# A rotated tile loop, maxima written by ScalarE, and row work moved across the ends of the attention and the FFN

## The reference, cut to what matters

```
def _L1_attn_ref(x, Wq, Wk, Wv, Wo, bo):           # 16 heads of 8, no mask
    s = einsum('bhtd,bhsd->bhts', q, k) / sqrt(8)
    m = max(s, axis=-1, keepdims=True)
    e = exp(s - m)
    out = einsum('bhts,bhsd->bhtd', e, v) / (sum(e, -1) + 1e-8)
    return out @ Wo.T + bo

def _L1_ffn_ref(x, ...):                           # DEPTH = 6
    for i in range(DEPTH):                         # 16 heads of 64, windows of 32 rows
        x = attn_layer(shift_tokens(x), Wqkv[i], q_scale[i], k_scale[i], Wo[i]) + x
        x = ffn_layer(shift_tokens(x), ln_g[i], ln_b[i], W1[i], b1[i], W2[i], b2[i]) + x
    return x
# attn_layer: q, k, v = split(x @ Wqkv); q, k = l2norm; rotary; local_attention
#             (softmax over the 64 keys of this and the last window); out @ Wo
# ffn_layer:  (x - mean) / sqrt(var + 1e-5) * g + b; a, gate = split(xn @ W1 + b1)
#             a * gelu(gate) @ W2 + b2
x = x + _L1_attn_ref(xn, ...) + _L1_ffn_ref(xn, ...)
```

## Time and profile before

| | us |
|---|---|
| median of three runs | 5288.02 (5263.25 to 5299.2) |
| the profiled execution | 5284.67 |
| its span | 5282.9 |
| PE, DVE, ACT, POOL busy in the span | 4393.2, 3444.4, 2413.4, 2446.8 |

### The profile page before, as it was taken

The page is one execution under the profiler, slowest core; times in us unless marked ns, Lnnn a source line. Parts: engine busy times, 40 slices in busy tenths (PEclk is TensorE's granted clock), DMA queues, the critical chain, the costliest instruction groups (busy, mean ns, idle before and its releaser), DMA issues. The chain is left out here.

```text
span 5282.9 us, 166221 instructions
## 1 busy us (share of the span) xinstructions
PE 4393.2 (83%) x69377; PEld 2783.1 (53%) x69377; DVE 3444.4 (65%) x5635; ACT 2413.4 (46%) x3236; POOL 2446.8 (46%) x3490
## 2 busy tenths in 40 slices
PE   3556548888799988999889998899988999889997
PEld 2333312322466655666556665566655666556664
DVE  6655656666477756777567775677756777467775
ACT  3434425556344443444444454444534445344453
POOL 1000021110567735666257772666726777176670
PEclk8788868888899999999899999999989999899998
DMA  0000011110222212222122221222202222022220
GB/s 28 0 0 0 0 35 41 44 48 30 65 71 71 71 42 57 71 71 71 34 61 70 69 74 31 67 71 71 70 26 73 70 68 74 25 71 71 71 69 17
DMA packets 187582, 273.42 MB, mean 52 GB/s; under 512 B 39248, under 2 KB 81616, under 8 KB 186192
## 3 DMA queue, kind: packets, MB, share of 16 engines
q1 hardware_dynamic: 186960, 263.67, 18.8%
HBM read 39.25 MB, written 8.39 MB: 9 GB/s over the span
## 5 line engine op out<-in xcount | busy, mean ns | idle before, releaser
L1331 ACT ACTIVATE ls_r<-PS 128x1024 f32<-128x1024 f32 x192 | 196.5, 1023 | 1065.6 <-PE PS L1209 1065.6
L1410 DVE TENSOR_TENSOR ls_a<-PS,TC 128x1024 f32<-128x1024 f32 x384 | 467.9, 1220 | 327.4 <-ACT ls_r L1331 326.7
L1209 PE MATMUL PS<-WQ,ls_xsT 128*128 128x512 f32 x768 | 458.0, 727 | 158.3 <-issue 146.2
L1110 POOL TENSOR_TENSOR ls_a<-ls_a,ls_q 128x1024 f32<-128x1024 f32 x192 | 453.1, 2360 | 241.9 <-DVE ls_q L1415 241.9
L1420 DVE TENSOR_REDUCE ls_ss<-ls_r 128x16 f32<-128x1024 f32 x384 | 466.4, 1214 | 94.2 <-ACT ls_r L1356 94.2
L1415 DVE TENSOR_TENSOR ls_q<-PS,TS 128x512 f32<-128x512 f32 x768 | 491.6, 682 | 0.0
L1130 POOL TENSOR_TENSOR ls_a<-ls_a,ls_q 128x1024 f32<-128x1024 f32 x192 | 454.8, 2369 | 0.0
L1266 PE MATMUL PS<-WO,ls_r 128*128 128x128 f32 x3072 | 404.1, 286 | 58.3 <-ACT ls_r L1359 58.3
L864 DVE TENSOR_REDUCE mxs<-PS 128x2 f32<-128x1024 f32 x256 | 307.6, 1221 | 215.2 <-PE PS L739 213.3
L1266 PEld LDWEIGHTS PS<-WO,ls_r 128*128 128x128 f32 x3072 | 367.0, 196 | 104.9 <-ACT ls_r L1359 104.9
L1217 PE MATMUL PS<-WQ,ls_xsT 128*128 128x512 f32 x768 | 394.7, 639 | 20.9 <-DVE ls_a L1410 20.9
(11 more groups left out here) (238 smaller groups left out, 8865.5 us busy)
## 6 DMA issues: line engine op xcount, KB each, us to landing
ls_vb<-ls_vt SPq DMA_DIRECT2D x1152, 130.0 KB
ls_vb<-ls_vt SPq DMA_DIRECT2D x672, 65.0 KB
ls_xs<-XL SPq DMA_DIRECT2D x42, 256.0 KB, 3.9
QT<-scratch SPq DMA_DIRECT2D x288, 32.0 KB
KT<-scratch SPq DMA_DIRECT2D x288, 32.0 KB
WQ<-wqkv SPq DMA_DIRECT2D x6, 1536.0 KB, 6.7
ls_vb<-ls_vz SPq DMA_DIRECT2D x96, 65.0 KB
scratch<-QP SPq DMA_DIRECT2D x24, 128.0 KB, 1.8
```

The costliest lines, as they stand in the source:

```text
L1110: pool.tensor_tensor(a4[:, 1], a4[:, 1], b4[:, 1], ALU.add).then_inc(s_ck, 1)
L1209: ins = pe.matmul(banks(K_BANK + c), rows, WQ[:, INNER + c * 512:INNER + c * 512 + 512], start=True, stop=True)
L1410: nc.vector.tensor_tensor(v4(A[fq])[:, a], src, tab, ALU.mult).then_inc(done, 1)
```

## The change

In the full attention, ACT writes the maxima itself. `MXT`, the `maxima` DMAs and their semaphore are gone; in their place stand four ACTIVATEs of three rows by 512, one a head, at steps 3 to 6. The maxima's rows move from 72 to 96 (`MROW`), and the second scores take 99 rows. `LAG` falls from 24 to 23; the sums over values stand at steps 1, 5, 9 and 13; the other steps that use bank 7 move back by two. DVE splits the maxima in four instructions, not five. POOL zeroes and sets `V2` later, behind its first `parts`, and sets one more piece of `KT` at the start.

In the layers, PE's `scores` and the K and V projections become `lead(front, back, order)`, which is called behind each slot. The order on PE stays as it was, but the loop now closes behind V instead of behind the scores. `HEAD` goes from 23 to 41, and the pass holds 2595 instructions. The last attention tile (`order == 4`) now holds what `ready(0)` did: PE's shifts ahead of the transposes of the exponentials, ACT's copies and squares, DVE's `centred(0)` ahead of the division and `scaled(0)` ahead of the residual. PE's `rows_up` for the next layer moves into the last `layer`, between the `W2` products of its two sequences; a first `rows_up` stands ahead of the loop over layers.

```
-HEAD = 23
+HEAD = 41
...
-                    pool.memset(KT[MROW - PAD:MROW, :, :, :], 1.0).then_inc(s_v0, 1)
+                    pool.memset(KT[MROW - PAD:MROW, :, :, :], 0.0).then_inc(s_v0, 1)
                     pool.wait_ge(s_v0, 3)
-                    pool.memset(V2[:, :, :, :, :], 0.0).then_inc(s_v0, 1)
-                    pool.wait_ge(s_v0, 4)
-                    pool.memset(V2[:, :, :, :, HD:HD + 1], 1.0)
+                    pool.memset(KT[MROW:P, :, :, :], 1.0)
...
-                                if m % TILES == 0:
-                                    pe.wait_ge(s_mr, 64 * (s + 1))
+                                if kt == 0:
+                                    pe.wait_ge(s_me, GH * s + g + 1)
...
-                            if k in (8, 10, 12, 14) and 0 <= t - 2 < GROUPS:
-                                s, kt = t - 2, (k - 8) // 2
+                            if k in (1, 5, 9, 13) and 0 <= t - 2 < GROUPS:
+                                s, kt = t - 2, k // 4
...
+                def turn(g, j):
+                    front = (g, j + 2) if j < 2 else (g + 1, j - 2)
+                    mid = (g, j + 1) if j < 3 else (g + 1, 0)
+                    return front + (g * NT + j + 2,), mid + (g * NT + j + 1,), (g, j, g * NT + j)
...
                 with loop(eng, 0, B - 1, head) as g:
                     for j in range(NT):
...
+                        slot(*turn(g, j), 3)
                         if j == 0:
                             stage(g + 1)
                         if j == 1:
                             prep(g + 1)
-                        scores(*mid, g * NT + j + 1)
...
+                        after = turn(g, j + 1) if j < 3 else turn(g + 1, 0)
+                        lead(after[0], after[2], 3)
...
+                        if order == 4:
+                            pe.wait_ge(s_aq, (l + 1) * TILES)
+                            pe.wait_ge(s_bq, (l + 1) * TILES)
+                            for a in range(2):
+                                pe.wait_ge(s_res, l * TILES + (a * PAIRS + 1) * NT + 1)
+                                shift(0, 2 + a, a * PAIRS, f_sh[a])
...
+                            if not more and s == 0:
+                                pe.wait_ge(s_xl[0], (l + 1) * PAIRS + 1)
+                                rows_up(XL[:, 0, 1:SLOTS, :])
```

More of the change, by code:

```diff
@@ L690, in _ @@
                     packed(1)
-                    for t in range(GROUPS + 1):
-                        if t:
-                            maxima(t - 1)
+                    for t in range(GROUPS):
                         if t % NG == 2 and t // NG + 1 < B:
@@ L988, in program, with tiles, last @@
             block = phase(ctx)
[L990 removed]
+            def tiles(eng, begin, slot, stage, prep, lead=lambda front, back, order: None, head=None):
+                def turn(g, j):
+                    front = (g, j + 2) if j < 2 else (g + 1, j - 2)
+                    mid = (g, j + 1) if j < 3 else (g + 1, 0)
+                    return front + (g * NT + j + 2,), mid + (g * NT + j + 1,), (g, j, g * NT + j)
+                def last(j):
+                    front, mid, back = turn(B - 1, j)
+                    return front if j < 2 else None, mid if j < 3 else None, back
                 begin()
+                lead((0, 0, 0), None, 1)
                 slot((0, 0, 0), None, None, 1)
+                lead((0, 1, 1), None, 2)
                 slot((0, 1, 1), (0, 0, 0), None, 2)
[L995 removed]
+                lead(turn(0, 0)[0], turn(0, 0)[2], 3)
                 with loop(eng, 0, B - 1, head) as g:
                     for j in range(NT):
[L998 to L1000 removed]
+                        slot(*turn(g, j), 3)
                         if j == 0:
@@ L1004, in tiles, with ahead @@
                             prep(g + 1)
-                        scores(*mid, g * NT + j + 1)
-                g = B - 1
+                        after = turn(g, j + 1) if j < 3 else turn(g + 1, 0)
+                        lead(after[0], after[2], 3)
                 for j in range(NT):
-                    slot((g, j + 2, g * NT + j + 2) if j < 2 else None, (g, j + 1, g * NT + j + 1) if j < 3 else None, (g, j, g * NT + j), 3)
+                    slot(*last(j), 3 if j < NT - 1 else 4)
                     if j < 3:
-                        scores(g, j + 1, g * NT + j + 1)
-            def ahead(eng, ready, layer):
-                ready(0)
+                        lead(last(j + 1)[0], last(j + 1)[2], 3)
+            def ahead(eng, layer):
                 with loop(eng, 0, PAIRS - 1) as p:
@@ L1218, in slot @@
                             ins.then_inc(s_v, 1)
+                    def slot(front, mid, back, order):
+                        if front:
+                            fb, ft, nf = front
+                            nf = l * TILES + nf + 1
+                            rows = xsT[0][:, XO - 1 + ft * P:XO - 1 + ft * P + P]
+                        if mid:
+                            mb, mt, nm = mid
+                            nm, mq = l * TILES + nm + 1, mt % 2
+                        if back:
+                            b, t, n = back
+                            n, q = l * TILES + n + 1, t % 2
+                        if order == 4:
+                            pe.wait_ge(s_aq, (l + 1) * TILES)
+                            pe.wait_ge(s_bq, (l + 1) * TILES)
+                            for a in range(2):
+                                pe.wait_ge(s_res, l * TILES + (a * PAIRS + 1) * NT + 1)
+                                shift(0, 2 + a, a * PAIRS, f_sh[a])
                         if back:
@@ L1267, in slot @@
                             ins.then_inc(s_w, 1)
-                    tiles(pe, begin, slot, lambda b: None, prep, scores, HEAD)
+                    tiles(pe, begin, slot, lambda b: None, prep, lead, HEAD)
                     def ready(p):
@@ L1331, in slot @@
                             act.activation(SQ[:, INNER:], banks(K_BANK, 2), ACT.Square).then_inc(s_sqk, 1)
+                        if order == 4:
+                            for a in range(2):
+                                act.wait_ge(f_sh[a], l * PAIRS + 1)
+                                act.activation(xs[a][:, :, D // 2:D], banks(2 + a)[:, 0:NT * D // 2].rearrange("p (t d) -> p t d", t=NT), ACT.Copy).then_inc(f_xu[a], 1)
                         if back:
@@ L1340, in slot @@
                                 act.activation(PRT[:, c * T:c * T + T], banks(PT_BANK[c]), ACT.Copy).then_inc(s_pte, 1)
+                        if order == 4:
+                            act.wait_ge(s_rdk, (l + 1) * TILES)
+                            for a in range(2):
+                                act.wait_ge(f_c[a], l * PAIRS + 1)
+                                act.activation(XQ[a], xs[a][:, :, :], ACT.Square).then_inc(f_sq[a], 1)
                         if front:
@@ L1390, in layer @@
                             ready(p + 1)
-                    ahead(act, ready, layer)
+                    ahead(act, layer)
             @block.vector
@@ L1437, in slot @@
                             sines(1, K_BANK, s_bk)
+                        if order == 4:
+                            centred(0)
                         if back:
@@ L1464, in slot @@
                             sines(0, Q_BANK, s_bq)
+                        if order == 4:
+                            scaled(0)
                         if back:
@@ L1528, in layer @@
                                                     R[s][:, T:2 * T].rearrange("p (t d) -> p t d", t=NT), ALU.add).then_inc(s_xl[s], 1)
[L1530 removed]
+                    ahead(dve, layer)
                     nc.vector.memset(mx[:, 0:1], 0.0).then_inc(free_ffn, 1)
```

175 lines of the change are left out of this document (82 added, 93 removed).

## The result

The changed kernel takes 4949.41 us (median of 4 runs, 4939.45 to 4959.88) against 5288.63 us (5263.25 to 5299.2) for the one before: ratio 0.9365, 95% interval 0.9327 to 0.9404. That is 339 us faster; the forecast was 4930 us, the range 4845 to 5105. The profiled execution took 4949.05 us with a span of 4947.5, 335.4 us less than the span before. The size came out, but not from the terms in the shares that the prediction gave them.

The account below looks back on a forecast made before the run. PE was taken to set the pace, through its waits and the lower clock after them. Terms 180 + 24 + 98 - 3 + 54 + 5 = 358 us won gave 4930 us against the median, range 4845 to 5105.

Parts of the forecast that it names:

- The loop's end and entry: Layers' loop on PE: moving the branch behind V wins 180 us at 36 loop ends and 24 us at 6 entries.
- 0.4 + 3.6 us of cover against 4.0: At the loop's end, 0.4 us of scores plus 3.6 us of K and V hide a 4.0 us code fetch.
- the second gap of 1.0 us: In the products with values after the loop's end: next code block 1.0 us late; 1.3 us of excess left in all.
- The fetch stays whole: Rival at the loop's branch: the 3.6 us stall moves behind V, loop's end and entry win nothing, 5134 us; chance 0.14.
- The full attention: Slots of the full attention: without the DMA's wait they fall from 18.07 to 14.9 us, 98 us won over 31 slots.
- PE may be two scores ahead, so I count half of it: Steps 3 to 6 of a slot: half of ACT's up to 1.2 us excess reaches PE, giving slots of 14.9 us.
- 14.37 us for a slot without waits: Full attention: a full-clock slot of 16.22 us less its 1.85 us wait for the DMA makes 14.37 us.
- The rival of the lower clock: Full attention: short waits for ACT in steps 3 to 6 keep PE at 1.2 GHz, +186 us, 5214 us; chance 0.03.
- The second block's start: Start of the second block: POOL's added memset of 32 rows delays DVE's normalisation, costing 3 us.
- The FFN's first rows: FFN's start: normalising inside the last tile removes PE's 9.9 us wait, 9.0 us a layer, 54 us, at best 59.
- the 0.9 us by which the last tile should grow: Last attention tile: growth taken off the 9.9 us won at the FFN's start, leaving 9.0 us a layer.
- The next layer's rows: From W2 products to the next K: earlier transposes and copies win 1 us in 5 places, 5 us, 0 to 12.

Follow-up runs that it names:

- the half rotation: The changed kernel with V moved from the end of `lead` to the head of `slot`, so the branch stands between K and V: 5012.42 us, ratio 0.9481.
- f1: The changed kernel with the FFN's first normalisation behind the last attention tile again, everything else as changed: 5034.57 us, ratio 0.9534.

## Why the prediction was right, point by point

- **The loop's end and entry** (180 + 24 = 204): 223 us measured (199 and 25), less 13 at the exit. The argument "0.4 + 3.6 us of cover against 4.0" held: the half rotation left 1.5 us. The mis-sized value is the second gap of 1.0 us that I kept in the excess: the second block was in time, and a loop end costs 0.5 us more than another tile on the mean (15.43 against 14.97), not 1.3.
- **What I did not see at all is the exit.** I took the branch for a place that PE passes one way. With K and V ahead of it, only 3 us of work are left behind it before the next boundary, and the block there is late by up to 2.7 us. With V behind the branch as well, or without the hint, that gap is gone.
- **The fetch stays whole**, a rival at 0.14, is out. By the Trainium skill ("Runtime: NRT & Kernel Launch", Instruction fetch mechanics) a branch outside the window must fetch before PE goes on, and code comes in blocks of 256. The blocks are there in the trace, in the gaps' places and the packets' size. The wait is there too: PE's sequencer stands in the branch for 2.8 us. But it need not reach PE, which works on what it has been given.
- **The full attention** (98) gave 35 us. The failing step is "PE may be two scores ahead, so I count half of it": of ACT's crowding in steps 3 to 6 PE felt all, 1.4 us in the slot shown against my 0.5 (14.9 less 14.37), and the sum at step 1, now right behind ACT's eviction, added 0.9 that the prediction did not name. The step before it was good: 14.37 us for a slot without waits; the kernel with two copies on DVE and the eviction earlier reached 14.52. The rival of the lower clock is half there: it falls in about half of the slots, for 1.5 us each.
- **The second block's start** (-3) was -3.3.
- **The FFN's first rows** (54, at best 59) gave 66 to 71 us. The 9.9 us went as told. The failing step is the 0.9 us by which the last tile should grow: it shrank. Its four shift products fill the wait for the exponentials (0.99 us against 2.10 and 0.66 in f1), and from the last scores to the W products it takes 13.0 us on the mean of the six layers against 13.9 before and 13.8 in f1.
- **The next layer's rows** (5, up to 12) gave 14 to 21 us. PE did not wait for the residual of sequence 0, and I left out that K and V then run at the higher clock.

So the loop's term was right by its argument, but that the total came within 20 us is luck: 63 us too much in the full attention met some 40 us too little in the layers.

## What to carry to other kernels

A loop as long as this one, 2594 instructions, costs at its back edge what the fetch takes less the work already issued behind the last block boundary (with the hint; behind the branch without it). Put long instructions there, start the loop early in a code block, and look at the exit as well as at the back edge. When a wait for a DMA is replaced by work on another engine, do the sum for the steps in which that work falls, not for the slot: ACT had two microseconds free a slot and was still late. And of two ways to end a wait, which is better depends on what else is crowded: with two copies on DVE, moving the one that is waited for (the eviction) gave more than moving the one that waits (slots of 14.52 against 15.27 us), and with all four on ACT it gave less (16.29 against 16.00).

## What the runs showed that I had not expected

- Slots of the code block matter as much as instructions: 244 us between `HEAD` 41 and 224, with the same instructions in the same order.
- After a jump three blocks can be late, one after the other, 2.9 and 4.4 us apart. The one long gap further on, 1.9 to 2.6 us in the tile after the exit when the branch stands between K and V, is not explained.
- An eviction of 3 rows by ACT takes 587 ns and one of 128 rows 593; on DVE the copy of 3 rows takes 692 ns.
- The gap at the exit varies between 0.8 and 3.1 us among the kernels with `HEAD = 41` and the branch behind V, from layer to layer and run to run with the same code. What decides it is open.
